# Codebook lookup by one-hot products: both table pieces in one PSUM bank, and folds of four slots in column quarters of TensorE

## The reference

```python
x = layernorm(x + attention(x, wq, wk, wv, wo))
Wg, Wu = codebook[idx_gate], codebook[idx_up]      # 2752 x 128 indices each -> 2752 x 1024
Wd = codebook[idx_down]                            # 1024 x 344 indices      -> 1024 x 2752
g, u = x @ Wg.T, x @ Wu.T
x = layernorm(x + (silu(g) * u) @ Wd.T)
```

## Time and profile before

| | |
|---|---|
| Times of the runs | 13,555.17, 13,550.04, 13,552.54 us (median 13,552.54) |
| The profiled execution | span 13,555.1 us, time 13,555.17 us |
| TensorE, matmuls busy | 7,807.1 us (58%), 29,072 records |
| VectorE busy | 4,989.8 us (37%) |
| ScalarE busy | 3,676.3 us (27%) |
| GpSimd busy | 5,592.7 us (41%) |
| Lookup products (L413) | 11,776 records, 3,120.5 us |
| Fold products (L424) | 1,472 records |
| Picks (L987) | 1,472 instructions, 1,032.2 us |

### The profile page before, as it was taken

One profiled execution on the slowest core, in us unless ns is written; L12 is line 12 of the kernel. 1 busy time (PEld: TensorE's weight loads), 2 busy tenths in 40 slices (PEclk: granted clock), 3 DMA queues, 4 the chain that ended last, 5 costly groups with the idle time before them and its releaser, 6 DMA issues. The chain is left out here.

```text
span 13555.1 us, 109335 instructions
## 1 busy us (share of the span) xinstructions
PE 7807.1 (58%) x29072; PEld 4545.7 (34%) x29072; DVE 4989.8 (37%) x11788; ACT 3676.3 (27%) x6498; POOL 5592.7 (41%) x5316
## 2 busy tenths in 40 slices
PE   4333333333320100010001999999999999999999
PEld 1111111111100000000000666656666666666665
DVE  1000000000000000000000777777878787777875
ACT  0000000000000000000000776555555555555553
POOL 7777777777777777777776000000000000000000
PEclk6555555555555555555555999999999999999999
DMA  2011101111110000000000112222222222222221
GB/s 63 13 16 16 16 14 28 16 13 13 13 13 8 8 6 8 7 7 8 7 8 5 28 27 68 72 57 62 65 61 65 64 62 64 62 65 61 65 61 52
DMA packets 472442, 462.10 MB, mean 34 GB/s; under 512 B 231120, under 2 KB 347728, under 8 KB 467536
## 3 DMA queue, kind: packets, MB, share of 16 engines
q10 hardware_dynamic: 287072, 396.73, 10.4%
q0 software_dynamic: 169984, 22.10, 3.7%
q1 hardware_dynamic: 14832, 36.84, 0.7%
HBM read 398.07 MB, written 57.15 MB: 34 GB/s over the span
## 5 line engine op out<-in xcount | busy, mean ns | idle before, releaser
L203 POOL DMA_INDIRECT raw<-in_codebook_dram,idx_sb x5312 | 5592.5, 1053 | 1825.3 <-issue 1822.2
L413 PE MATMUL ps<-onehot,table 128*128 128x512 f32 x11776 | 3120.5, 416 | 68.8 <-DVE picked L987 48.3
L979 DVE TENSOR_SCALAR_CACHE_REDUCE onehot<-arena,small 128x512 fp32r<-128x512 f32 x3685 | 2514.6, 742 | 914.9 <-PE ps L413 900.1
L413 PEld LDWEIGHTS ps<-onehot,table 128*128 128x128 f32 x11776 | 2196.0, 188 | 912.2 <-issue 373.1
L272 PE MATMUL ps<-big,arena 128*128 128x512 f32 x1024 | 959.4, 958 | 1609.1 <-issue 1593.1
L745 ACT ACTIVATE onehot<-arena,small 128x512 fp32r<-128x512 f32 x2211 | 1434.9, 713 | 1208.4 <-PE ps L413 1130.4
L749 ACT ACTIVATE onehot<-onehot,small 128x512 fp32r<-128x512 f32 x2211 | 1425.0, 708 | 0.0
L893 DVE TENSOR_REDUCE small<-ps 128x1 f32<-128x384 f32 (+7 forms) x512 | 376.3, 753 | 2608.9 <-remote 2378.4
L441 PE MATMUL ps<-big,arena 128*128 128x512 f32 (+1 forms) x2816 | 1281.2, 592 | 1.3 <-DVE big L971 1.3
L320 PE MATMUL ps<-id_sb,arena 128*128 128x128 f32 x2304 | 385.5, 301 | 1324.7 <-issue 1272.9
L619 ACT COPY arena<-ps 128x512 f32<-128x512 f32 (+3 forms) x768 | 335.2, 484 | 2950.3 <-remote 2039.8
(11 more groups left out here) (70 smaller groups left out, 4227.3 us busy)
## 6 DMA issues: line engine op xcount, KB each, us to landing
arena<-code_low ACTq DMA_DIRECT2D x738, 256.0 KB, 3.4
arena<-code_high ACTq DMA_DIRECT2D x738, 128.0 KB, 3.3
raw<-in_codebook_dram,idx_sb POOLq DMA_INDIRECT x5312
gathered_units<-raw SPq DMA_DIRECT2D x40, 512.0 KB
arena<-gathered_units ACTq DMA_DIRECT2D x20, 1024.0 KB, 6.6
queries_keys<-arena ACTq DMA_DIRECT2D x16, 1024.0 KB
arena<-queries_keys ACTq DMA_DIRECT2D x32, 512.0 KB
big<-in_xT_dram ACTq DMA_DIRECT2D x4, 2048.0 KB, 19.4
```

The lines of the kernel that those rows point to most:

```text
L203: pool.indirect_dma_start(raw[:, s, n, :], None, codebook, bass.IndirectOffsetOnAxis(ap=idx_sb[:, s, n:n + 1], axis=0),).then_inc(gathered ...
L413: last = mm(ps[:, bank + c, :], table[:, k, c, :], onehot[:, k, :], start=(k == 0), stop=(k == KLO - 1))
L979: dve.tensor_scalar(onehot[:, k, :], lo_sb[:, s % 2, :], kp_sb[:, k:k + 1], None, ALU.is_equal, ALU.add, accum_out=hits[:, k:k + 1]).then_ ...
```

## The change

Both pieces of the table are summed in one bank (4 or 5, by turns of the slot), so that there is one pick for each slot, written in float32 into one of four places of `picked`. The fold is made once for four slots: four float32 products of 128x32 by 128x512, each with its own picked tile and its own quarter of the PSUM partitions (and so of TensorE's columns), and with the same window of a smaller `sel`. The fold of a group of four slots is issued behind `look_up` of the slot that follows the group; `pick` of the first slot of a group waits for it, and `look_up(s)` waits for the pick of slot s-2. The cast of `sel` is gone. The codes are laid out so that the four slots of a group belong to four quarters. Cut to its core:

```diff
-WIDE = P + (JT - 1) * CS
+QUAD = 4
+QUADS = SLOTS // QUAD
+COLS = P // QUAD
+WIDE = COLS + (COLS // CS - 1) * CS
...
-        picked = nc.alloc_sbuf_tensor_at("picked", [P, 2, PIECES, N], F32R, offset=arena_at + 44 * 1024)
+        picked = nc.alloc_sbuf_tensor_at("picked", [P, QUAD, N], F32, offset=arena_at + 44 * 1024)
...
-        sel_sb = nc.alloc_sbuf_tensor_at("sel", [P, WIDE], F32R, offset=arena_at + 60 * 1024)
-        sel_raw = hT[:, 0:WIDE]
+        sel_sb = kb(60, 1)[:, 0:WIDE]
...
                     if k == 0:
-                        past(pe, masked, first * PIECES + PIECES * (s - held))
+                        past(pe, masked, first + (s - 1))
                     for c in range(PIECES):
-                        last = mm(ps[:, bank + c, :], table[:, k, c, :], onehot[:, k, :],
-                                  start=(k == 0), stop=(k == KLO - 1))
+                        last = mm(ps[:, 4 + s % 2, :], table[:, k, c, :], onehot[:, k, :],
+                                  start=(k == 0 and c == 0), stop=(k == KLO - 1 and c == PIECES - 1))
                     last.then_inc(onehot_used, 1)
...
-            def fold(first, unit, s):
-
-                half, j = divmod(s, JT)
-                pe.wait_ge(masked, first * PIECES + PIECES * (s + 1))
-                if j == 0:
+            def fold(unit, f):
+
+                half, turn_in = divmod(f, COLS // CS)
+                pe.wait_ge(masked, unit * SLOTS + QUAD * (f + 1))
+                if turn_in == 0:
                     past(pe, taken, unit)
-                for c in range(PIECES):
-                    last = mm(ps[:, 6 + half, :], sel_sb[:, WIDE - P - j * CS:WIDE - j * CS], picked[:, s % 2, c, :],
-                              start=(j == 0 and c == 0), stop=(j == JT - 1 and c == PIECES - 1))
+                for g in range(QUAD):
+                    last = mm(ps[g * COLS:(g + 1) * COLS, 6 + half, :], sel_sb[:, WIDE - COLS - turn_in * CS:WIDE - turn_in * CS],
+                              picked[:, g, :], start=(turn_in == 0), stop=(turn_in == COLS // CS - 1))
                 last.then_inc(folded, 1)
...
                 for s in range(SLOTS):
                     look_up(first, s)
-                    if s:
-                        fold(first, unit, s - 1)
-                    else:
-                        fold(first - SLOTS, unit - 1, SLOTS - 1)
+                    if s % QUAD == 0:
+                        if s:
+                            fold(unit, s // QUAD - 1)
+                        else:
+                            fold(unit - 1, QUADS - 1)
...
-            def pick(first, s, bank):
-                dve.wait_ge(onehot_used, first * KLO + (s + 1) * KLO)
-                dve.wait_ge(hi_in[s % 4], first * 4 + (s // 4 + 1) * 16)
-                past(dve, folded, first + (s - 1))
-                for c in range(PIECES):
-                    dve.scalar_tensor_tensor(picked[:, s % 2, c, :], hi_sb[:, s % 4, :], hi_row_sb, ps[:, bank + c, :],
-                                             ALU.is_equal, ALU.mult).then_inc(masked, 1)
+            def pick(unit, s):
+                dve.wait_ge(onehot_used, unit * (SLOTS * KLO) + (s + 1) * KLO)
+                dve.wait_ge(hi_in[s % 4], unit * (SLOTS * 4) + (s // 4 + 1) * 16)
+                past(dve, folded, unit * QUADS + s // QUAD)
+                dve.scalar_tensor_tensor(picked[:, s % QUAD, :], hi_sb[:, s % 4, :], hi_row_sb, ps[:, 4 + s % 2, :],
+                                         ALU.is_equal, ALU.mult).then_inc(masked, 1)
...
-            dve.wait_ge(sel_in, 16)
-            dve.tensor_copy(sel_sb[:, :], sel_raw).then_inc(sel_ready, 1)
...
-    codes[0:NLOOK] = [w.reshape(2, 4, P, JT).transpose(0, 3, 1, 2) for w in first + whole[0:NPK]]
+    codes[0:NLOOK] = [w.reshape(2, 4, P, QUAD, JT // QUAD).transpose(0, 4, 3, 1, 2).reshape(2, JT, 4, P)
+                      for w in first + whole[0:NPK]]
```

## The result

The changed kernel takes **13,371.8 us** (median of four runs, 13,368.2 to 13,373.1) against 13,553.9 for the kernel before beside it: ratio 0.9866, 95% interval 0.9852 to 0.988, 182 us less. Forecast were 13,381 us and 172 us less. The profiled execution has a span of 13,371.3 us.

What follows compares the result with a forecast made beforehand. The prediction took the pace of TensorE's products, behind about 8 ms the change leaves alone, as the bound. Folds 118, stalls 52 and cast 2.5 made 172 us off the median 13,552.5: 13,381 us, range 13,340 to 13,445.

Steps and rivals of the forecast that it cites:

- Part 1: TensorE's folds: one fold of four side-by-side float32 products takes 1.23 us, replacing four folds; 118 us off the path.
- the chance of 0.70: Chance given to the forecast case, in which a fold's four tiles run at once in 0.86 us.
- Part 2: Look-up products all into one bank: at most 35 us dearer, taken as nothing; a gain excluded.
- Part 3: One pick and two banks end look-up stalls: 22 us in the blocks, 30 us at the loop's steps, together 52 us.
- the entry into the first step: Start of the loop's first step: counted as one of 20 stalls of 1.5 us that end.
- Part 4: No cast of the fold matrix before VectorE's first one-hot: 2.5 us off, once.
- Part 5: Pick of every fourth slot waits on VectorE for the fold behind its look-up: taken as costing nothing.
- two at a time: Rival: only two column groups are fed at once, a fold 0.86 us longer, 158 us more, 13,539 us; chance 0.08.
- none beside another: Rival: fold passes in quarters run one after another, 3.80 us a fold, 473 us more, 13,854 us; chance 0.06.
- The staggered fold: Rival: the fold's four tiles don't start together, a fold 0.22 us longer, 40 us more, 13,421 us; chance 0.12.
- the rival of the new wait: Rival: the pick waiting for the fold holds up the next products, 121 us come back, 13,502 us; chance 0.04.

Runs made afterwards that it cites:

- x11: The changed kernel with every second gather left out (missing entries zeros), on the third chip: 6744.7 us, ratio 0.9736 to the kernel before.
- x1: The changed kernel with the fold's four products at full width, each adding to the whole bank: 13,789.1 us, ratio 1.0173 to the kernel before.
- x4: The changed kernel with every pick done twice, two banks kept: 13,374.1 us.
- x2: The changed kernel with the fold in two halves of 64 columns, two slots to a half: 13,535.2 us, ratio 0.9986 to the kernel before.
- x5: The changed kernel with a fold of two slots behind every second look-up, on the second chip: 6955.6 us, ratio 1.0039 to the kernel before.
- x3: The changed kernel with one bank for the look-up, which waits for the pick of the slot before: 13,391.8 us.
- x6: The changed kernel with seven of eight folds one slot later, on the second chip: 6878.6 us, ratio 0.9935 to the kernel before.
- x10: The changed kernel with ScalarE's four silu passes one slot later, on the third chip: 6890.0 us, ratio 0.9955 to the kernel before.
- x7: The changed kernel with ScalarE's four silu passes one slot later, on the second chip: 6885.9 us, ratio 0.9938 to the kernel before.
- x9: The changed kernel unedited, run again on the third chip: 6881.8 us, ratio 0.9935 to the kernel before.

## Why the prediction was right

**What bounds it**: right for the chip whose trace was read. TensorE is at 99.6% in the loop and follows the sum. The prediction took the first 8 ms as a fixed block; that holds there, but on the other two chips the block is 1.6 ms, and GpSimd, idle from 7.4 ms on in the trace that was read, gathers nearly to the end. The range would have missed there, and nothing in the prediction says for which chip it holds. Gathers that take 7.4 ms (6.8 on the other chips) are longer than all the rest of the work where the attention is quick (6745 us in x11), but that the attention can be quick no row of before shows.

**The sum**: 172 us forecast, 182 measured. The terms below come to 179 of the 183.8 us between the two profiles; the other 5 are an attention that ended 2.4 us earlier with unchanged instructions (between the profiles of x1 to x4 the start of the first look-up also differs, by up to 2.6 us) and 2.2 us behind the loop that no experiment takes apart. So the nearness of 13,372 to 13,381 is earned in the terms, and no two of them had to cancel.

**Part 1, the folds**: forecast 118 us. Measured per fold 1.19 us in place of 1.23 (0.99 with the way in, 0.20 out), 0.67 less than four folds of before: 176 x 0.67 = 118 us, and 7 us in the 64-channel tile, 125 in all. That four tiles run together was a step beyond the rows, which had two, and the chance of 0.70 put it as a choice; x1 and x2 settle it. The price of 0.35 us for the changes of width, taken from the 64-channel tile, was 0.33. The Trainium skill has 2.38 times for three column tiles ("TensorE: Matmul & The Clock Gate", Measured speedup vs the span model); at that efficiency a fold would have been, as an estimate, 0.22 us longer. It isn't: the pass is 4.0 times as quick as in x1 (0.86 against 3.43 us), and the whole fold with its changes of width 2.9 times (1.19 against 3.43). Its rule that a change of tiling mode drains the engine ("TensorEngine Tiling (Array Packing)", Key Properties) agrees with these runs: at full width (x1) nothing is added to the eight records or behind them, in quarters 0.13 us on the way in and 0.20 on the way out, and x5 pays that twice as often.

**Part 2, one bank**: right, 3.65 us for 16 products.

**Part 3, the stalls**: forecast 52 us (22 in the blocks, 30 in the steps). Measured 39.4 - 24 x 0.67 = 23 in the blocks, and 130.2 - 152 x 0.67 = 28 in the loop; the entry into the first step, which I had priced like the others, gave nothing. The sizes hold, the reason was half wrong: I gave both to the pick of two slots before. x3 shows that nearly only the blocks need the second bank. The stall of the steps ends either way: with one bank and a single pick (x3), and with two banks and every pick done twice (x4). The longer fold of slot 0 is there in both; what it does by itself, no run shows.

**Part 4, the cast**: 2.5 us forecast; both engines now write their first one-hot at 8251.06. The other 2.4 of the 4.8 us in the table are an attention that ended that much earlier in this profile, with unchanged instructions.

**Part 5, the new wait**: free, as forecast; VectorE's idle time before its picks is 156 us in all, 142 of it behind folds, and in the trace no instruction of TensorE waits for a pick. x6 shows the edge, one slot further.

**The rivals**: "two at a time" and "none beside another" are x2 and x1, at 13,535 and 13,789 us where 13,539 and 13,854 were worked out. The second rival has its records one after another in quarters and pays for the change of width; x1 has them at full width and doesn't, which is the difference of 65 us. The staggered fold is ruled out by the timeline, where the four records of a pass start 7 ns apart, and the rival of the new wait by part 5.

**What stays open**: why the engines issue so slowly during the gathers on the first chip (below), the later last gather of x10 and x7, and what x7 brings on the first chip, where 49 us are due by its slots. On the other two it is no faster than the changed kernel, and only x11, which leaves work out, is.

## What to carry to other kernels

If the output of a product has few rows, collect as many of them as fit beside each other in the array and issue them together: the group costs one product and one change of width (here 0.86 + 0.33 us, with two tiles in it as with four), so it pays by the number of tiles in it. A pick that makes room for a later product can wait for a product on TensorE at no cost, as long as nothing that TensorE needs within that time stands behind it on its own engine. And hold the sum of each engine's work against the whole time, not only against the stage in which one trace shows it: 7 ms of gathers that lie hidden beside a slow stage set the end as soon as that stage is quick.

## What the runs showed of the hardware that was not expected

**Two kinds of chip.** In the first two sets of runs the projections and the attention took 8.25 ms, in the last two 1.62 ms, for the same instructions; the gathers took 7.4 and 6.8 ms. The last two sets ran on two different chips. Whether the kind belongs to the chip or to something else that differed between the sets isn't shown. A stretch of the projections in the timeline of the changed kernel, on the first chip and then on the other kind (x9):

```profile
1999.10 1.01 PE L274 MATMUL ps<-big,arena 128*128 128x512 f32 x1 [1.79 <-issue]
1999.40 1.09 POOL L205 DMA_INDIRECT raw<-in_codebook_dram,idx_sb  x1 [0.30 <-issue]
2000.50 0.29 PEld L274 LDWEIGHTS ps<-big,arena 128*128 128x128 f32 x1 [2.51 <-issue]
...
2001.90 1.01 PE L274 MATMUL ps<-big,arena 128*128 128x512 f32 x1 [1.79 <-issue]
```
```profile
399.50 4.88 PE L274 MATMUL ps<-big,arena 128*128 128x512 f32 x11
399.72 0.94 POOL L205 DMA_INDIRECT raw<-in_codebook_dram,idx_sb  x1 [0.30 <-issue]
...
400.97 0.94 POOL L205 DMA_INDIRECT raw<-in_codebook_dram,idx_sb  x1 [0.30 <-issue]
```

In the first, TensorE starts one instruction for each gather of 1.40 us, a weight load and a product by turns, at the moment a gather ends; in the second it starts a record every 0.43 us while the gathers pass every 1.25 us. The 1600 us of "issue" in which L274 waits in the page of the first are these. The slices of the span of the changed kernel on the first chip show how long this lasts:

```profile
PE   4333333333331000000100799999999999999999
POOL 7777777777777777777777100000000000000000
PEclk6555555555555555555555899999999999999999
```

The last gather ends at 7416.8 us. In the 3716 us before that TensorE has 1306 records of products, and in the 200 us from 7500 us on 1931, still in the attention. Three quarters of the records of this part run in its last 0.83 ms. So it is beside running gathers that the engines are slow on this chip, and behind them they are quick here too. TensorE's granted clock is 0.50 (1.2 GHz) from 100 us to the last gather, while the engine is busy for a quarter of the time, and 1.00 (2.4 GHz) from 7500 us on, with the engine busy throughout. What makes the engines issue in step with the gathers on the one kind of chip and not on the other was not tried: x11, with half the gathers, ran only on a chip of the quick kind.
